# Doubling the SBUF scratch for the descriptors of Pool's transfers in a graph layer with a routed feed-forward layer

## The reference

```
n = layernorm(x)
h = layernorm(n) * gamma + beta
x = x + n + relu((adj @ h) @ W_rel + b_rel + h @ W_root)     # graph layer

n = layernorm(x)
scores = n @ Wg.T + bg                                       # 8 experts
the two best experts of each row, softmax over their two scores
x = x + n + sum over the two: p * (relu(n @ W1[e].T + b1[e]) @ W2[e].T + b2[e])
```

## Time and profile before

| | us |
|---|---|
| median of the timed runs | 627.26 |
| lowest, highest | 627.03, 627.95 |
| span of the profiled execution | 878.1 |
| busy in it: PE, PEld | 471.1, 395.1 |
| busy in it: DVE, ACT, POOL | 385.6, 237.7, 272.6 |
| busy in it: POOL line 298, line 311 | 123.2, 121.3 |

### The profile page before, as it was taken

The page is one execution under the profiler, slowest core; times in us unless marked ns, Lnnn a source line. Parts: engine busy times, 40 slices in busy tenths (PEclk is TensorE's granted clock), DMA queues, the critical chain, the costliest instruction groups (busy, mean ns, idle before and its releaser), DMA issues.

```text
span 878.1 us, 14976 instructions
## 1 busy us (share of the span) xinstructions
PE 471.1 (54%) x4776; PEld 395.1 (45%) x4777; DVE 385.6 (44%) x1146; ACT 237.7 (27%) x467; POOL 272.6 (31%) x268
## 2 busy tenths in 40 slices
PE   0613243441799997401099997201299951899500
PEld 0613233330688886201088886100188840688400
DVE  2979933830454667200044668000055620456622
ACT  0413100210356554000056553000044410344200
POOL 3053373067000000777400001777300067000274
PEclk9955575565799999655589999655599975899955
DMA  9980012011112112211112112111122222221341
GB/s 346 416 287 1 19 51 64 6 58 51 43 44 78 56 57 67 68 54 51 33 44 78 57 57 82 52 54 51 27 73 72 72 78 53 74 73 54 135 132 57
DMA packets 32173, 70.78 MB, mean 81 GB/s; under 512 B 14458, under 2 KB 14714, under 8 KB 31364
## 3 DMA queue, kind: packets, MB, share of 16 engines
q1 hardware_dynamic: 21520, 37.66, 13.0%
q0 software_dynamic: 8192, 16.79, 6.6%
q10 hardware_dynamic: 2420, 15.77, 4.4%
HBM read 32.45 MB, written 37.75 MB: 80 GB/s over the span
## 4 chain that ended last, share of the span: by engine, by line
PE 42%; issue 20%; another core or an unknown queue 13%; DVE 13%; DMA 4%; ACT 3%; POOL 3%; SPq 2%; ACTq 0%; DVEq 0%; POOLq 0%
PE PH L876 14%; PE PY L893 13%; PE PH L872 5%; POOL YG L311 3%; DMA ADJ<-in_adj 3%; PE PX L859 2%; ACT N L695 1%; PE PY L886 1%; SPq L223 1%; ACT N L677 1%; PE PA L824 1%; DVE VARN L377 1%; DVE MDIF L376 1%; DVE N L442 1%
## 5 line engine op out<-in xcount | busy, mean ns | idle before, releaser
L298 POOL DMA_INDIRECT rows<-XHL,IDX x128 | 123.2, 962 | 347.1 <-DVE IDX L515 309.3
L540 DVE SCALAR_TENSOR_TENSOR HL<-PH,HH 128x512 f16<-128x512 f32 x192 | 129.8, 689 | 207.0 <-ACT HH L726 114.1
L726 ACT ACTIVATE HH<-PH 128x512 f16<-128x512 f32 x192 | 113.6, 596 | 263.1 <-PE PH L876 107.9
L311 POOL DMA_INDIRECT YG<-yrows,IDX x128 | 121.3, 948 | 202.7 <-DMA yrows<-YB 164.3
L876 PE MATMUL PH<-XT,W1H 128*128 128x256 f16 x768 | 144.3, 281 | 22.8 <-issue 22.6
L893 PE MATMUL PY<-W2H,HL 128*128 x768 | 131.0, 223 | 31.8 <-issue 31.8
L893 PE MATMUL PY<-W2H,HH 128*128 x768 | 131.1, 223 | 25.3 <-issue 25.3
L893 PE MATMUL PY<-W2L,HH 128*128 x768 | 109.3, 223 | 42.1 <-issue 42.1
L535 DVE COPY XT<-PX 128x512 f16<-128x512 f16 x96 | 40.5, 422 | 168.6 <-issue 63.1
L876 PE MATMUL PH<-XT,W1L 128*128 128x256 f16 x384 | 107.8, 281 | 12.3 <-issue 12.3
L876 PEld LDWEIGHTS PH<-XT,W1H 128*128 x768 | 76.3, 100 | 55.8 <-issue 32.9
(11 more groups left out here) (154 smaller groups left out, 559.8 us busy)
## 6 DMA issues: line engine op xcount, KB each, us to landing
rows<-XB ACTq DMA_DIRECT2D x4, 3072.0 KB, 29.8
XB<-rows SPq DMA_DIRECT2D x32, 384.0 KB
yrows<-YB SPq DMA_DIRECT2D x32, 384.0 KB, 2.3
out<-X SPq DMA_DIRECT2D x16, 256.0 KB
X<-in_x SPq DMA_DIRECT2D x3, 1024.0 KB, 28.2
YG<-in_w ACTq DMA_DIRECT2D x1, 2048.0 KB, 9.6
ADJ<-in_adj SPq DMA_DIRECT2D x32, 64.0 KB, 3.8
YG<-in_w SPq DMA_DIRECT2D x1, 2048.0 KB, 29.7
```

What stands on the lines that cost most here:

```text
L298: nc.gpsimd.indirect_dma_start(rows[q], bass.IndirectOffsetOnAxis(ap=IDX[:, col:col + 1], axis=0), XHL[:, src:src + 2 * P].bitcast(F32), N ...
L311: nc.gpsimd.indirect_dma_start(YG[q % 2][:, dst:dst + P], None, yrows[q], bass.IndirectOffsetOnAxis(ap=IDX[:, col:col + 1], axis=0)).then_ ...
L540: nc.vector.scalar_tensor_tensor(HL[:, at:at + 2 * BW], PH[h][:, :], 0.0, HH[:, at:at + 2 * BW], ALU.max, ALU.subtract).then_inc((loa_made ...
L726: nc.scalar.activation(HH[:, at:at + 2 * BW], PH[h][:, :], ACT.Relu).then_inc((hia_made, hib_made)[h][j], 1)
```

## The change

The constructor of the program is given a scratch of 32,768 bytes of each partition in place of the default of 16,384. Every SBUF tensor stands 16,384 bytes further up in its partition. Nothing else of the program changes; 17 empty lines at the top of the file go, so that line numbers are lower by 17.

```diff
@@ -999,7 +982,7 @@
         "b2": c(a["L0_ffn_b2"].reshape(1, E * P)),
         "kf": kf, "kh": kh,
     }
-    nc = bacc.Bacc("TRN2", target_bir_lowering=False, num_devices=1)
+    nc = bacc.Bacc("TRN2", target_bir_lowering=False, num_devices=1, dynamic_dma_scratch_size=32768)
     aps = {n: nc.dram_tensor("in_" + n, v.shape, mybir.dt.from_np(v.dtype), kind="ExternalInput").ap()
            for n, v in arrays.items()}
     out = nc.dram_tensor("out", (P, TILES * P), F32, kind="ExternalOutput").ap()
```

## The result

Runs of the two kernels taken side by side: 631.96 us for the changed kernel (20 runs, 628.25 to 634.19) against 627.15 us (20 runs, 624.45 to 632.33). The ratio of the two is 1.0054, with a 95% interval of 1.0030 to 1.0077: 3.4 us more, within 1.9 to 4.8. It is not the quotient of the two medians, which would be 1.0077 or 4.8 us; ratios and intervals in this text are all of the first kind, and the medians stand beside them. The forecast was no change, 625.7 to 628.8 us. The profiled execution of the changed kernel took 630.88 us and has a span of 629.1 us.

A forecast was written before the change was run, and what follows sets the result against it. It took the timed runs as bound by the preparation and first two graph quarters, the PE-bound passes and the last burst of 32 gathers. More room and higher tensors summed to 0 + 0, leaving 627.3 us, range 625.7 to 628.8.

The forecast's parts named there:

- the sum for more room: Last burst of 32 gathers: gain from less waiting for descriptor room, between 0 and 9.6 us, taken as 0.
- Rival B: At the start, before ADJ's clearing: setting up the scratch costs by its size, 3.6 us slower, 630.9 us; chance 0.04.
- More room gains nothing: Pool's 256 indirect transfers: none waits a whole microsecond for descriptor room, so doubled room saves 0 us.
- Tensors higher up cost nothing: All SBUF tensors 16,384 bytes higher: instruction times don't depend on operand addresses, so 0 us.
- the bound of 3 us: Matmuls of lines 893 and 876: at most one nanosecond each from shifted addresses, about 3 us either way.
- The crawl: Inside Pool's bursts PE does about 1 matmul per us, not 10; claimed for the profiled execution only, not timed runs.
- The ring estimate: Pool's descriptor ring: 16,384 bytes hold 113 transfers, coming round at 114 and 228, with doubled scratch at 228 alone.
- The chance of 0.87 for no change: Whole kernel: no effect, time 627.3 us, in nearly all of it within 0.2%; faster had 0.07, slower 0.06.

The follow-up runs named there:

- e3: Default scratch, but an unused tensor of 16,384 bytes of each partition allocated first, against the kernel before: 881.32 us, ratio 0.9998.
- e13: Whole kernel with 12,288 bytes of scratch, against the kernel before with 16,384: one run of 627.97 us beside 629.68 us.
- e14: Whole kernel with 20,480 bytes of scratch, against the kernel before with 16,384: one run of 631.32 us beside 629.68 us.
- the small kernel: Computation left out; sixteen blocks of 0 to 256 gathers, each ending in Pool's DRAIN. With 16,384 bytes: 9.19 us at 112 gathers, 0.61 at 120.

## Why the prediction was wrong

**The step that failed** is the sum for more room: "on the path stands the last burst alone", with 0 as its value. It took the last store as the end of the path. Between the store's issue at 872.23 and the span's end at 878.1 there were 5.9 us, for which the sum has no term. What stands there is Pool's DRAIN: 7.905 us with 16,384 bytes and 10.518 us with 32,768, so 2.61 us where the sum has 0. The room was asked only what it could save in waiting, not what Pool does at the end with all that it still keeps. The trace held the row of 7,905 ns (source view of line 62), and SP's wait of 3.7 us at line 62 pointed at it.

**Rival B had the right sign and the wrong place and cause.** "Setting up the scratch costs by its size" was put at the start, at 3.6 us. It is at the end, 2.61 us, and goes by transfers, not by bytes: doubling from 16,384 to 32,768 adds 32 kept transfers, from 8,192 to 16,384 it adds 40.

**More room gains nothing: right.** No transfer waited for room in the profile of the kernel before; even 8,192 bytes show no such gap, and 4,096 only four.

**Tensors higher up cost nothing: right**, by e3 (0.9998, 0.9980 to 1.0017). (Lines 893 and 876 have 3,456 matmuls between them, not 3,072; the bound of 3 us would have been 3.5.)

**The crawl: wrong.** I took it for a mark of the profiled execution. On four chips every timed run of the kernel before takes 878 to 889 us, and the profiled execution of the changed kernel has a span of 629.1 us and a time of 630.88. That the timed runs at 627 us have no crawl was right. But from the crawling profile I had also read that all bursts but the last lie beside PE's work. Without the crawl they don't all: scatter 3, gather 1 and gather 2 run together as one burst of 121 us, and DVE waits for gather 1 before it can start the last quarter's passes:

```profile
487.48 0.42 DVE L518 COPY XT<-PX 128x512 f16<-128x512 f16 x1 [10.39 <-DMA YG<-yrows,IDX]
```

It changed nothing here: the same wait is 10.1 us with 12,288 and with 20,480 bytes (e13, e14), and the step of the transfers is the same in all.

**The ring estimate** of 113 transfers, from "DMA: Bandwidth & Descriptors" of the Trainium skill (sections "Terms" and "The descriptor swizzle"), is what the small kernel shows: the gap stands before the 114th gather, 112 gathers are all walked and 120 leave 7. In the whole kernel the row at 114 showed nothing because the transfers to be struck off had landed; by the rule nothing falls on 228, since only 32 or 8 go at a time.

**The chance of 0.87 for no change** rested on the bounds of two effects that I could name. A third that I couldn't had been given nothing; 0.04 for B was what was left for it.

The Trainium skill has a sentence on such rows: "VectorE: DVE Perf Modes" (section "The DRAIN you can't avoid") calls the DRAINs of a program's start and end boilerplate of about 12 ns on all engines. SP's 12 and 13 ns here agree; Pool's 2,025 to 10,518 ns do not, nor does DVE's row at the same line with 1,174 ns. Whether the page means the rows of a block's end is left open by it; for these the measurement decides.

## What to carry to other kernels

Follow the path to the span's last row, through the barrier: the queue rows of the line that closes the block belong to it, and they are in no list of busy time. A kernel that ends soon after Pool's transfers, as this one does, pays 82 ns for each that Pool still keeps; here a smaller scratch, or Pool reaching its DRAIN earlier, makes that cheaper, down to where another engine joins last (SP, with 8,192 bytes and less). When a resource is made larger, ask also what is done once for all that it holds.

## What the runs showed of the hardware that I had not expected

- Pool's DRAIN at a block's end: 0.05 us and 82 ns for each kept transfer of 128 rows, though it has landed. At most 128 are kept, or as many as the scratch has room for (28, 56, 113 with 4,096, 8,192, 16,384 bytes). The list is inferred from these times and from the gaps.
- Striking off goes oldest first, by whole groups with one semaphore, and waits where the group hasn't landed: 2.1 us before transfer 29 with 4,096 bytes.
- One program takes 627 us on one chip (or at one time) and 880 us on others. In the slower case PE gets about one matmul in a microsecond through while Pool issues transfers, against ten otherwise. What makes the two cases differ was not found.
